# Relation layer of a four-layer graph network: waits between the indirect gathers of a half-turn

## The chip, the cores and the metric

The kernel runs on one NeuronCore of a Trainium2 chip as one program. The metric is the device time of an execution in microseconds; the median of three executions of the kernel before is 9646.02 us.

## The reference

Four graph layers follow one another on 6250 nodes of 64 features and 206250 edges that are sorted by destination. Each is added to its input. The change is in the last, the relation layer:

```python
    def _L3_gnn_ref(x, edge_index, edge_type, W_rel, W_self, b_self):
        ...
        out = x @ W_self.T + b_self
        src = x[edge_index[0]]
        msg = jnp.zeros((src.shape[0], W_rel.shape[1]), dtype=x.dtype)
        for r in range(W_rel.shape[0]):
            msg = msg + jnp.where((edge_type == r)[:, None], src @ W_rel[r].T, 0.0)
        out = out.at[edge_index[1]].add(msg)
        return jax.nn.relu(out)
    ...
    h = jnp.maximum(_layernorm(x, axis=-1), 0.0)
    x = x + _L3_gnn_ref(h, edge_index, edge_type_3, L3_gnn_W_rel, L3_gnn_W_self, L3_gnn_b_self)
```

## The kernel before

An earlier stage has written `relation_table` to HBM: for each node and each of three relations one row of 64 floats, the node's features times that relation's matrix. The relation layer then needs, for each edge, one row of that table, and running sums of those rows along the edges of each partition, so that a node's sum can be read at its last edge.

The 206250 edges lie as 128 partitions by T columns. A **half-turn** handles HALF = 26 columns, in one of two buffers (h = 0 or 1); a loop turn has two half-turns, and LP = 31 turns make 62 half-turns. Five engines run side by side in one block, each with a loop of its own, joined by semaphores alone:

- **POOL** (GpSimd) waits until ACT has staged the indices of the half-turn (`s_idx`), then issues NGA = 21 indirect gathers, one per column, each of 128 rows of 256 bytes, into `rows_l3_h` (line 3027). All 21 count on one semaphore, `s_rows[h]`, and are issued without a wait between them.
- The other ND = 5 columns are not gathered. **PE** makes them by dense one-hot products: five tiles of 21 matmuls each (line 3232), with small transposes and products by the relations' weights between them (lines 3242 and 3252), that **DVE** masks and sums (lines 3144 to 3172).
- **ACT** builds the one-hots (lines 2980 and 2983). In `body` it waits for the 21 gathers and for the dense rows, turns the 26 columns by feature into PSUM (lines 2993 to 2995), and only then stages the indices of the half-turn two on (line 2967). So the gathers of half-turn n + 2 start when half-turn n has been turned, and half-turn n + 1's gathers lie a whole period ahead of their use.
- **DVE** scans the turned columns (line 3179); ACT copies the result back (line 3003); **SP** stores it to `running_sums`, 832 KB per half-turn (line 3048), and loads the rows of codes for coming one-hots (line 3043).

Two other places gather in the same way. The mean layer (second of the four; line 1295) gathers from `h_table` in half-turns of 12 columns, GP = 12, and it already waits, ahead of each gather, for the landing of the gather two back:

```python
                        for u in range(GP):
                            if u > 1:
                                e.wait_ge(s_grow[s][u % 2], i * 8 * GP + 16 * (u // 2))
                                e.sem_inc(s_gpace, 1)
                            e.indirect_dma_start(grow[s][:, u, :], None, h1_d,
```

The attention layer (third; line 1600) gathers without such waits.

`retire(sems)` clears and frees semaphores behind a barrier of all engines. The first layer's semaphores (`l0_...`) are never freed in the kernel before.

Of the kernel before, what the change touches and what calls it, by code (L numbers as in the profile page):

```python
# [23 lines left out]
NACC = 4  # L24
# [122 lines left out]
def build(nc, x, src, dst, edge_attr, edge_type, w0a, b0a, w0b, b0b, w1, b1, watt, att_s, att_d, batt, wf1, bf1, wf2,  # L147
# [57 lines left out]
    with top:  # L205
# [3 lines left out]
        def sem(name, into=None):  # L209
            if into is None:  # L210
                return top.enter_context(nc.semaphore(name))
            into.append(nc.alloc_semaphore(name))
            return into[-1]

        def retire(sems):
            nc.clear_and_free_semaphores(sems)
            nc.all_engine_barrier()
# [384 lines left out]
        with ExitStack() as ctx:  # L602
# [22 lines left out]
            def borrow(k, n, dt=f32):  # L625
# [15 lines left out]
            s_attr = [sem(f"l0_attr{h}") for h in range(2)]  # L641
            s_stage, s_psrc, s_eq, s_sum, s_val, s_hot, s_hist, s_dup, s_tgt, s_vfree, s_acc = (
                sem(f"l0_{n}") for n in ("staged", "src_rows", "equal", "summed", "values", "onehots", "hist",
                                         "dup", "targets", "val_free", "pace"))
            s_high, s_left, s_spread, s_z, s_dig, s_digits = (
                sem(f"l0_{n}") for n in ("high_parts", "rests", "spread", "z_added", "digits_staged", "digits"))
            s_add = [sem(f"l0_acc{k}") for k in range(NACC)]
            s_init, s_tail, s_pack = sem("l0_init"), sem("l0_tail"), sem("l0_packed")
            s_away, s_gap = sem("l0_digits_negated"), sem("l0_digit_distances")
            s_srow = [sem(f"l0_src_rows_loaded{h}") for h in range(2)]  # L650
            s_turn, s_turnc, s_turnst = (sem(f"l0_{n}") for n in ("src_turned", "src_turned_copied", "src_turned_stored"))
# [335 lines left out]
        with ExitStack() as ctx:  # L987
# [205 lines left out]
            retire(retired0)  # L1193
# [1692 lines left out]
        with ExitStack() as ctx:  # L2886
# [39 lines left out]
            s_rows = [sem(f"l3_rows{h}", l3_sems) for h in range(2)]  # L2926
# [36 lines left out]
            with nc.Block() as block:  # L2963
                @block.scalar
                def _(e):
# [20 lines left out]
                    def body(i, h, more):  # L2986
# [3 lines left out]
                        e.wait_ge(s_rows[h], i * 16 * NGA + 16 * NGA)  # L2990
# [27 lines left out]
                @block.gpsimd  # L3018
                def _(e):
                    with e.Fori(0, LP) as i:  # L3020
                        for h in range(2):
                            hh = i * 2 + h

                            e.wait_ge(s_idx, hh + 1)
                            e.sem_inc(s_pace, 1)
                            for r in range(NGA):
                                e.indirect_dma_start(g[h][:, r, :], None, y3_d,  # L3027
                                                     bass.IndirectOffsetOnAxis(ap=idx[h][:, r:r + 1], axis=0))\
                                 .then_inc(s_rows[h], 16)
# [335 lines left out]
```

## Time and profile before

| | us |
|---|---|
| median of three executions | 9646.02 (9627.27 to 9649.23) |
| span of the profiled execution | 9754.5 |
| relation layer: first to last gather start of line 3027 | 7024.7 to 9642.7 |
| POOL busy, whole span | 5337.6 |
| PE matmul busy, whole span | 6607.5 |

The profiled execution has no time beside its span; its span is 108.5 us, 1.1%, over the median of the unprofiled executions. POOL's busy time counts an indirect gather for some 0.94 us, the time in which its descriptors are made; the transfer goes on after it.

### The profile page before, as it was taken

Reading aid. Unit: us, or ns where it says so; the run is one execution under the profiler, and the core shown is the slowest. Engines: PE = TensorE matmul, PEld = TensorE weight load, DVE = VectorE, ACT = ScalarE, POOL = GpSimd, SP = SyncE. Lnnn points to the kernel's source line nnn. Section 1 sums busy time; section 2 is a strip of 40 time slices with the busy share of each in tenths; the row PEclk is TensorE's granted clock in tenths of the full one; section 3 lists DMA queues with packets and bytes.
Section 4 is the critical chain, followed back from the end, with each engine's and each line's share of the span. In section 5 each row is a group of like instructions: output and inputs, shape, how many; then the busy total and the mean of one; then the engine's idle time right before and its main releaser. Section 6 shows DMA issues by size and latency. Waiting matters only on the chain. (4 is left out here: it accounts for less than half of the span.)

```text
span 9754.5 us, 145261 instructions
## 1 busy us (share of the span) xinstructions
PE 6607.5 (68%) x38830; PEld 4546.4 (47%) x38831; DVE 6236.8 (64%) x16834; ACT 4860.4 (50%) x11241; POOL 5337.6 (55%) x4893
## 2 busy tenths in 40 slices
PE   6988888875888852555555555557767666666665
PEld 3545545544777741445454444557533333333332
DVE  7999999986888832666676666668633333333333
ACT  5877777754777721333333333333334444444442
POOL 5888888873555545455555545551344444444444
PEclk9999999987888955555655555555577788888777
DMA  5444444441111112222222222222111111111111
GB/s 120 73 75 70 72 75 70 72 76 41 21 20 21 21 41 38 44 43 45 45 46 44 45 43 45 44 45 75 51 38 43 45 46 46 46 46 43 41 41 46
DMA packets 626461, 487.11 MB, mean 50 GB/s; under 512 B 513289, under 2 KB 530030, under 8 KB 616344
## 3 DMA queue, kind: packets, MB, share of 16 engines
q0 software_dynamic: 281600, 185.95, 15.9%
q1 hardware_dynamic: 342455, 293.43, 10.2%
q10 hardware_dynamic: 2304, 6.55, 0.3%
q8 instruction: 41, 0.67, 0.0%
q14 instruction: 61, 0.50, 0.0%
HBM read 303.43 MB, written 182.13 MB: 50 GB/s over the span
## 5 line engine op out<-in xcount | busy, mean ns | idle before, releaser
L1600 POOL DMA_INDIRECT tile_rows<-att_row_table,src_by_tile x1620 | 1528.4, 943 | 1413.6 <-PE banks L2269 763.7
L3027 POOL DMA_INDIRECT rows_l<-relation_table,idx x1302 | 1246.4, 957 | 1390.5 <-ACT idx L2967 1012.3
L976 POOL DMA_INDIRECT acc<-val,idx x1116 | 1722.6, 1544 | 378.9 <-issue 319.9
L3232 PE MATMUL banks<-h_parts,dense_onehot 128*128 128x448 bf16 x6510 | 1511.3, 383 | 553.0 <-issue 518.2
L2269 PE MATMUL banks<-tile_rows,prob 128*128 x4032 | 910.4, 402 | 1386.3 <-ACT prob L2210 595.5
L747 PE MATMUL banks<-part 128*128 128x490 bf16 (+1 forms) x7440 | 1569.6, 366 | 217.9 <-DVE part L830 209.8
L2269 PEld LDWEIGHTS banks<-tile_rows,prob 128*128 128x128 f32 x4032 | 831.8, 307 | 1480.6 <-issue 1480.3
L3232 PEld LDWEIGHTS banks<-h_parts,dense_onehot 128*128 128x128 bf16 x6510 | 643.0, 103 | 1334.6 <-issue 854.1
L747 PEld LDWEIGHTS banks<-part 128*128 128x128 bf16 x7440 | 694.3, 97 | 996.0 <-DVE part L830 270.4
L3144 DVE TENSOR_TENSOR h_nodes<-banks,dense_mask_j 128x448 f32<-128x448 f32 x310 | 192.9, 622 | 1476.3 <-remote 910.1
L2210 ACT COPY prob<-banks 128x1024 f32<-128x1024 f32 x252 | 255.0, 1012 | 1307.8 <-DMA quad_sums<-run 1076.4
L2318 DVE TENSOR_TENSOR banks<-banks,piece_att_dst 128x1024 f32<-128x1024 f32 x252 | 310.2, 1231 | 895.9 <-remote 877.9
L1295 POOL DMA_INDIRECT gathered_rows<-h_table,gathered_index x600 | 575.8, 960 | 545.3 <-issue 295.7
L906 ACT ACTIVATE digit_distance<-iota_row,dst_digits_negated 128x128 bf16<-128x128 f32 (+1 forms) x3224 | 868.7, 357 | 2.2 <-ACT dst_digits_negated L895 0.2
L1350 DVE TENSOR_SCALAR hot_src_lo<-columns_bf,codes 128x128 bf16<-128x128 bf16 x2300 | 613.6, 269 | 134.0 <-ACT codes L1414 59.4
L1453 ACT CAST counts<-banks 128x784 bf16<-128x784 f32 x650 | 522.2, 815 | 301.2 <-PE banks L1502 188.2
L830 DVE SCALAR_TENSOR_TENSOR part<-banks,src_digits,part 128x490 bf16<-128x490 f32 x992 | 671.2, 718 | 0.0
L1351 DVE TENSOR_SCALAR hot_code<-columns_bf,codes 128x196 bf16<-128x196 bf16 x2300 | 647.6, 285 | 0.0
L3003 ACT COPY run<-sums_by_feature 128x1664 f32<-128x1664 f32 x62 | 213.4, 3441 | 866.5 <-DVE sums_by_feature L3179 562.7
L2367 DVE SCALAR_TENSOR_TENSOR kept_l<-kept_l,fade,banks 128x65 f32<-128x65 f32 x2016 | 565.7, 281 | 117.9 <-issue 58.2
L1527 PE MATMUL banks<-counts,h_parts 128*128 128x208 bf16 x4900 | 630.0, 275 | 4.4 <-issue 4.2
L2196 ACT ACTIVATE edge_logit<-banks 128x1024 f32<-128x1024 f32 x252 | 257.8, 1023 | 569.8 <-DVE banks L2318 383.3
(449 smaller groups left out, 12370.0 us busy)
## 6 DMA issues: line engine op xcount, KB each, us to landing
src_rows<-src_by_column SPq DMA_DIRECT2D x63, 1152.0 KB
piece_sums<-kept_l SPq DMA_DIRECT2D x252, 264.0 KB
running_sums<-run SPq DMA_DIRECT2D x62, 832.0 KB
attr<-in_edge_attr SPq DMA_DIRECT2D x61, 624.0 KB
tile_rows<-att_row_table,src_by_tile POOLq DMA_INDIRECT x1620
rows_l<-relation_table,idx POOLq DMA_INDIRECT x1302
dense_code_rows<-src_by_column SPq DMA_DIRECT2D x62, 320.0 KB
acc<-val,idx POOLq DMA_INDIRECT x1116
```

The source lines that it names most:

```text
L747: last = e.matmul(ps[a][:, 0:ZW[a]], place0[(h * NZ + m) % 2][:, a, :], spread0[(h * NZ + m) % 2][n].rearrange("p b f -> p (b f)")[:, 0:ZW ...
L830: last = e.scalar_tensor_tensor(spread0[b][n], bc(ps[7][:, 0:ZB].unsqueeze(2), [P, ZB, W0]), dig[h][:, m, ZA:ZA + 1], bc(t.unsqueeze(1), [ ...
L906: last = e.activation(gap[n][:, r - a, :], iota[:, 0:w], ACT.Square, bias=away[n][:, r:r + 1])
L976: e.indirect_dma_start(acc_d[k], bass.IndirectOffsetOnAxis(ap=idx[h][:, r:r + 1], axis=0), val[h][:, r, :], None, compute_op=ALU.add).then ...
L1295: e.indirect_dma_start(grow[s][:, u, :], None, h1_d, bass.IndirectOffsetOnAxis(ap=gidx[s][:, u:u + 1], axis=0))\
L1350: e.tensor_scalar(hlo[slot(q)][:, u, :], cols[:, 0:P], code[s][:, 0, n:n + 1], None, ALU.is_equal)
L1351: last = e.tensor_scalar(hcd[slot(q)][:, u, :], cols[:, :], code[s][:, 1, n:n + 1], None, ALU.is_equal)
L1527: last = e.matmul(ps[4 + 1 - s][:, 0:BN * HT], parts4[:, m // 2, m % 2 * 2 * D:(m % 2 + 1) * 2 * D], table[1 - s][:, :, m // 2 * BN:(m // ...
L1600: e.indirect_dma_start(to, None, hx_d, bass.IndirectOffsetOnAxis(ap=src_col[:, t:t + 1], axis=0))\
L2269: last = e.matmul(summed(r), prob[u % 2][:, r, :], flat[:, bass.ds(cols[r], W1)], start=True, stop=True)
L3027: e.indirect_dma_start(g[h][:, r, :], None, y3_d, bass.IndirectOffsetOnAxis(ap=idx[h][:, r:r + 1], axis=0))\
L3232: last = e.matmul(ps[4 + b][:, 0:WJ], hot[h][:, k, m * P:(m + 1) * P], parts3[:, n, k * WJ:(k + 1) * WJ], start=(k == 0 and n == 0), stop= ...
```

## The change

In the relation layer POOL waits, ahead of gathers 2 to 20 of a half-turn, until the gather two back has landed. For this the gathers of a half-turn count in turn on two semaphores, even ones on `s_rows[h][0]` (11 of the 21) and odd ones on `s_rows[h][1]` (10). ACT's wait for all 21 becomes two waits. To have semaphores enough, those of the first layer are now collected in a list and freed with others at the end of that layer's last block.

```diff
-            s_rows = [sem(f"l3_rows{h}", l3_sems) for h in range(2)]
+            s_rows = [[sem(f"l3_rows{h}_{n}", l3_sems) for n in range(2)] for h in range(2)]
+            LANDED = [-(-NGA // 2), NGA // 2]
...
-                        e.wait_ge(s_rows[h], i * 16 * NGA + 16 * NGA)
+                        for n in range(2):
+                            e.wait_ge(s_rows[h][n], i * 16 * LANDED[n] + 16 * LANDED[n])
...
                             for r in range(NGA):
+                                if r > 1:
+                                    e.wait_ge(s_rows[h][r % 2], i * 16 * LANDED[r % 2] + 16 * (r // 2))
+                                    e.sem_inc(s_pace, 1)
                                 e.indirect_dma_start(g[h][:, r, :], None, y3_d,
                                                      bass.IndirectOffsetOnAxis(ap=idx[h][:, r:r + 1], axis=0))\
-                                 .then_inc(s_rows[h], 16)
+                                 .then_inc(s_rows[h][r % 2], 16)
...
-            s_attr = [sem(f"l0_attr{h}") for h in range(2)]
+            l0_sems = []
+            s_attr = [sem(f"l0_attr{h}", l0_sems) for h in range(2)]
...
-            retire(retired0)
+            retire(l0_sems + retired0)
```

On POOL, the relation layer's loop turn reads before as follows (the destination, then the table and the indices; `x20` stands for twenty more of the same):

```order
L3020 ISA
L3027 DMA rows_l3_0<-relation_table,idx0 128x64 [waits l3_staged]
L3027 DMA rows_l3_0<-relation_table,idx0 128x64 x20
L3024 REGISTER_ALU
L3027 DMA rows_l3_1<-relation_table,idx1 128x64 [waits l3_staged]
L3027 DMA rows_l3_1<-relation_table,idx1 128x64 x20
L3020 REGISTER_ALU
L3020 COMPARE_AND_BRANCH
```

The start of the same loop turn on POOL now:

```order
L3023 ISA
L3033 DMA rows_l3_0<-relation_table,idx0 128x64 [waits l3_staged]
L3033 DMA rows_l3_0<-relation_table,idx0 128x64
L3031 ISA
L3033 DMA rows_l3_0<-relation_table,idx0 128x64 [waits l3_rows0_0]
L3031 ISA
L3033 DMA rows_l3_0<-relation_table,idx0 128x64 [waits l3_rows0_1]
L3031 REGISTER_ALU
L3033 DMA rows_l3_0<-relation_table,idx0 128x64 [waits l3_rows0_0]
```

The first two gathers of a half-turn follow each other as before; each later one waits for a landing, and in half-turns of buffer 0 a register instruction stands between them as well. The gathers of buffer 1 have the waits without the register instruction.

On ACT, at `body` of buffer 0, before:

```order
L2983 ACTIVATE dense_onehot0<-h_nodes,dense_one 128x1280 [waits l3_gaps]
L2990 ISA
L2991 ISA [waits l3_rows0]
L2992 REGISTER_ALU [waits l3_dense_rows]
L2993 COPY banks<-sums_by_feature 128x64 [waits l3_scanned]
```

and now:

```order
L2985 ACTIVATE dense_onehot0<-h_nodes,dense_one 128x1280 [waits l3_gaps]
L2993 ISA
L2993 ISA [waits l3_rows0_0]
L2994 ISA [waits l3_rows0_1]
L2995 REGISTER_ALU [waits l3_dense_rows]
L2996 COPY banks<-sums_by_feature 128x64 [waits l3_scanned]
```

One wait has become two, at the same place; what follows is as it was. PE, DVE and SP have the same instructions as before in this layer.

## Rows read from the trace of the kernel before

**Rows 1.** The page's span and its queues of instruction loads.
```profile
span 9754.5 us, 145261 instructions
...
q8 instruction: 41, 0.67, 0.0%
q14 instruction: 61, 0.50, 0.0%
```

**Rows 2.** The gathers by source line: count, min/median/max ns, first and last start.
```profile
L3027 POOL DMA_INDIRECT rows_l<-relation_table,idx x1302: 938/944/7818, 7024.7 to 9642.7; - x186
```

**Rows 3.** What PE waited for, 7105 to 9640 us: total, times, longest.
```profile
PE banks L3232 <- issue: 506.7, 323, 3.2
```

**Rows 4.** Timeline of PE in one half-turn: start, length, count, idle before.
```profile
7667.36 4.15 PE L3232 MATMUL banks<-h_parts,dense_onehot 128*128 128x448 bf16 x21
7671.43 0.65 PE L3242 MATMUL banks<-ident,h_nodes 128*64 128x128 f32 x4
...
7687.29 1.69 PE L3232 MATMUL banks<-h_parts,dense_onehot 128*128 128x448 bf16 x8
7690.24 0.35 PE L3232 MATMUL banks<-h_parts,dense_onehot 128*128 128x448 bf16 x1 [1.26 <-issue]
...
7704.98 2.34 PE L3232 MATMUL banks<-h_parts,dense_onehot 128*128 128x448 bf16 x6 [0.17 <-issue]
7708.19 0.59 PE L3252 MATMUL banks<-w_again,h_nodes 64*128 64x192 f32 x2 [0.87 <-DVE h_nodes L3156]
7708.71 4.14 PE L3232 MATMUL banks<-h_parts,dense_onehot 128*128 128x448 bf16 x21
```

**Rows 5.** Timeline of POOL, the same half-turn.
```profile
7675.23 0.94 POOL L3027 DMA_INDIRECT rows_l<-relation_table,idx  x1 [16.91 <-ACT idx L2967]
7676.48 0.94 POOL L3027 DMA_INDIRECT rows_l<-relation_table,idx  x1 [0.30 <-issue]
...
7700.18 0.94 POOL L3027 DMA_INDIRECT rows_l<-relation_table,idx  x1 [0.30 <-issue]
7716.26 0.94 POOL L3027 DMA_INDIRECT rows_l<-relation_table,idx  x1 [15.13 <-ACT idx L2967]
```

**Rows 6.** Windows: PE, PEld, DVE, ACT, POOL busy, clock, DMA share, GB/s.
```profile
7681.00:7689.00 8.00, 7.64 (x40) 3.89 (x39) 4.57 (x4) 0.00 (x0) 5.87 (x8) 1.00 0.14 25
7690.00:7696.00 6.00, 1.23 (x3) 0.20 (x2) 0.05 (x1) 5.88 (x4) 4.58 (x5) 0.79 0.38 125
```

**Rows 7.** Timeline of PE, then of POOL, in other half-turns.
```profile
8600.16 0.35 PE L3232 MATMUL banks<-h_parts,dense_onehot 128*128 128x448 bf16 x1 [0.38 <-issue]
...
8615.67 3.23 PE L3232 MATMUL banks<-h_parts,dense_onehot 128*128 128x448 bf16 x9 [0.87 <-issue]
...
9299.51 6.61 PE L3232 MATMUL banks<-h_parts,dense_onehot 128*128 128x448 bf16 x21
...
8585.89 0.94 POOL L3027 DMA_INDIRECT rows_l<-relation_table,idx  x1 [15.73 <-ACT idx L2967]
```

**Rows 8.** What PE waited for in the mean layer, 2326 to 3450 us.
```profile
PE banks L1502 <- issue: 23.8, 27, 3.0
PE banks L1527 <- issue: 4.2, 11, 0.9
```

**Rows 9.** Timeline of POOL in the mean layer.
```profile
2911.67 0.95 POOL L1295 DMA_INDIRECT gathered_rows<-h_table,gathered_index  x1 [8.77 <-ACT gathered_index L1410]
2912.92 0.94 POOL L1295 DMA_INDIRECT gathered_rows<-h_table,gathered_index  x1 [0.31 <-issue]
2914.86 0.94 POOL L1295 DMA_INDIRECT gathered_rows<-h_table,gathered_index  x1 [0.99 <-DMA gathered_rows<-h_table,gathered_index]
...
2930.45 0.94 POOL L1295 DMA_INDIRECT gathered_rows<-h_table,gathered_index  x1 [0.30 <-issue]
```

**Rows 10.** Windows in the mean layer, columns as in rows 6.
```profile
2380.00:2460.00 80.00, 70.33 (x673) 61.10 (x672) 70.30 (x386) 59.18 (x116) 45.59 (x48) 0.91 0.12 23
```

**Rows 11.** Window over 59 half-turns, columns as in rows 6.
```profile
7125.00:9617.00 2492.00, 1675.52 (x7423) 779.07 (x7422) 894.42 (x1188) 1098.30 (x948) 1174.01 (x1244) 0.80 0.17 44
```

**Rows 12.** The page's DMA issues: count and KB each.
```profile
running_sums<-run SPq DMA_DIRECT2D x62, 832.0 KB
```

More of the change, by code:

```diff
@@ L640, in build @@
             src_z = src0f[:, 0:T].rearrange("p (h r) -> p h r", r=HALF)[:, :, HS:HALF]
-            s_attr = [sem(f"l0_attr{h}") for h in range(2)]
+            l0_sems = []
+            s_attr = [sem(f"l0_attr{h}", l0_sems) for h in range(2)]
             s_stage, s_psrc, s_eq, s_sum, s_val, s_hot, s_hist, s_dup, s_tgt, s_vfree, s_acc = (
-                sem(f"l0_{n}") for n in ("staged", "src_rows", "equal", "summed", "values", "onehots", "hist",
+                sem(f"l0_{n}", l0_sems) for n in ("staged", "src_rows", "equal", "summed", "values", "onehots", "hist",
                                          "dup", "targets", "val_free", "pace"))
             s_high, s_left, s_spread, s_z, s_dig, s_digits = (
[L646 to L651, printed above, removed]
+                sem(f"l0_{n}", l0_sems) for n in ("high_parts", "rests", "spread", "z_added", "digits_staged", "digits"))
+            s_add = [sem(f"l0_acc{k}", l0_sems) for k in range(NACC)]
+            s_init, s_tail, s_pack = (sem(f"l0_{n}", l0_sems) for n in ("init", "tail", "packed"))
+            s_away, s_gap = (sem(f"l0_{n}", l0_sems) for n in ("digits_negated", "digit_distances"))
+            s_srow = [sem(f"l0_src_rows_loaded{h}", l0_sems) for h in range(2)]
+            s_turn, s_turnc, s_turnst = (sem(f"l0_{n}", l0_sems) for n in ("src_turned", "src_turned_copied", "src_turned_stored"))
             assert TT * P >= T + HALF > (TT - 1) * P and 12 < TT < 17 and TT * P <= HS * P
```

## The prediction
> **What bounds the kernel now.** I read first where the relation layer lies and how long a half-turn takes, then the timelines of PE and POOL over one half-turn, then the same two engines in the mean layer, which already has the waits that the change adds.
>
> The span of the profiled execution is 9754.5 us [rows 1]. The 1302 gathers of line 3027 are 62 half-turns of 21; first and last start are 7024.7 and 9642.7 us [rows 2]. The last half-turn's first gather lies 20 steps of 1.25 us (25 us) ahead of the last one, so 61 periods fill 2593 us: 42.5 us per half-turn. The one of the timeline is typical: its second tile starts at 7667.36 and the next half-turn's at 7708.71 [rows 4], 41.35 us.
>
> In that time PE is the engine that the others wait for, but it does not work all the time. From 7667.36 to 7687.29 four of its five tiles go by with what stands between them: 19.9 us, each tile some 4.07 us from its start to the next row's [rows 4]. The fifth starts at 7687.29 and is over only at 7708.19, 20.9 us where 4.1 would do. In it single matmuls stand 2 to 3 us apart, and the idle time ahead of them is put down to "issue": PE waited for nothing that the profile shows. Inside a tile the program has no wait at all. Over the layer that is 506.7 us of idle in 323 gaps, a little more than five a half-turn [rows 3], and more goes into the wide steps between them. Without the crawl PE's half-turn would be 41.35 - 20.9 + 4.1 = 24.6 us.
>
> What goes on beside the crawl: POOL starts its gathers at 7675.23, steps by 1.25 us, and starts the last at 7700.18 [rows 5]. The crawl begins 15 us after the first gather (7690.24) and ends 4.8 us after the start of the last (7704.98) [rows 4, 5]. Another half-turn, whose first gather starts at 8585.89, has its first gap ahead of 8600.16 and its last ahead of 8615.67 [rows 7]: 14.3 and 29.8 us after the first gather, where the one above has 15.0 and 29.75. The place in PE's program is not the same in the two (after the 8th matmul of the tile there, after the 5th here). So it goes by the gathers' time, not by PE's code. The DMA engines are not full at its onset: their share is 0.14 before, and 0.38 in the crawl because SP's store of 832 KB [rows 12] falls into it [rows 6]. The granted clock falls after PE has gone quiet (1.00, then 0.79, then 0.50), that is from 2.4 to 1.2 GHz, so the clock is a result and makes the recovery a little slower.
>
> **What the mean layer says.** There POOL already waits for the landing of the gather two back. In its whole loop the matmuls of line 1527 lost 4.2 us to "issue", those of line 1502 23.8 us [rows 8], though PE is fed as densely (673 matmuls in 80 us, busy 70.3, with 48 gathers beside them [rows 10], so 1.67 us per gather, kept up over the 80 us). There is no crawl. The gathers are of the same kind: 128 rows of 256 bytes and 0.94 us each.
>
> **The change part by part.** *The waits on POOL.* In the mean layer a gather whose landing is waited for starts 3.19 us after the one two back (2911.67 to 2914.86), and from the first gather of one half-turn to the first of the next are 18.78 us for 12 gathers [rows 9]: five pairs and two unpaced steps of 1.25 us, so a pair takes (18.78 - 2.5) / 5 = 3.26 us. With 21 gathers there are ten pairs and one step: 10 x 3.26 + 1.25 = 33.85 us for POOL per half-turn, where it was 26.2. The register instructions stand in the mean layer too and are in that pair. Queued behind the waits are only the other gathers.
>
> *What the store adds.* SP's store of 832 KB takes DMA time in the relation layer, and the mean layer has nothing of its size. The window with the store shows 125 GB/s over 6 us [rows 6]; a gather caught in it lands later, and then POOL waits longer. Bounds: nothing, if it only fills idle engines; or 5 us, if no gather lands during the store (832 KB at 125 GB/s is 6.7 us, less the 1.6 that a gather takes anyway). I take 2 us, since the share in that window is 0.38 and so mostly free. POOL then needs 35.85 us a half-turn.
>
> *Whether anybody waits for the later gathers.* The gathers of half-turn n + 2 start when n has been turned; POOL now idles 15 to 17 us ahead of each half-turn for ACT's indices [rows 5], so its own 7.6 to 9.6 us more are covered even at today's period, and the rows are needed a whole period after their start. If the period shrinks, that cover goes: POOL becomes the bound at 35.85 us, with its indices staged well ahead.
>
> *What is removed.* If the crawl goes, as in the mean layer, PE needs 24.6 us, ACT 1098 / 59 = 18.6 us and DVE 894 / 59 = 15.2 us of work per half-turn [rows 11], all below 35.85. PE would then idle some 10 us a half-turn, and the clock would fall there; a tile at the lower clock takes 6.61 us instead of 4.15 [rows 4, 7]; with three of five tiles slow PE is at 24.6 + 3 x 2.46 = 32 us, still below POOL. So the new period is POOL's, 35.85 us.
>
> *The semaphores of the first layer.* They are cleared with others behind a barrier that is there before: at most a microsecond. ACT's second wait passes with the first: nothing.
>
> **The sum.** The first two half-turns are bound by the layer's start and I leave them out; 59 periods go from 42.3 us (what is left of the 2593 us) to 35.85: 6.45 x 59 = 380 us less. The span would be 9754.5 - 380 = 9374 us. The profiled span stands 1.1% over the median, so off the median go 376 us: 9646 - 376 = 9270 us. That the unprofiled time is only 108 us shorter also says that the crawl (62 times some 16 us) is not made by profiling.
>
> **The rule that speaks against it.** By POOL's rows alone the gathers are hidden already, with 15 us to spare [rows 5], and a wait between them gains nothing. The Trainium skill, "DMA: Bandwidth & Descriptors", section on rules for kernel authors, says to issue a DMA early and wait on its semaphore late, so that its fixed cost overlaps; by it the change can only cost, and at best nothing. The mean layer's rows decide it for me the other way.
>
> **Rivals.**
> 1. *The crawl goes by the gathers' rate, and is only shortened.* At 1.25 us a step it starts after 11 or 12 gathers; if it builds up whenever gathers come faster than about 1.7 us apart, the paced stream of 1.71 us (35.85 / 21) is near that edge, and a short crawl or slower gathers put the half-turn at 37.5 to 41 us. For it: the onset needs a backlog. Against: 1.67 us per gather over 80 us in the mean layer [rows 10]. Saving 1.3 to 4.8 us x 59: 9363 to 9570 us, say 9450. Chance 0.13.
> 2. *The crawl is PE's own code loading and has nothing to do with the gathers.* A loop turn of PE is taken back at a branch, and the code behind it would have to come again. Then the half-turn stays at 42 us and the waits hide in POOL's idle time: 9646 us. Against: the crawl's place follows the gathers, and the queues of instruction loads hold 41 and 61 packets in the whole span [rows 1], not some for each of 62 half-turns. The skill's page "Runtime: NRT & Kernel Launch", section on instruction fetch, says that a taken branch to code outside the window forces such a load; no row here shows one in this loop. Chance 0.05.
> 3. *Slower: the crawl lasts as long as gathers are in flight, from some 14 us after the first.* Then POOL's longer burst makes it longer: 33.85 - 26.2 = 7.6 us more crawl, of which PE gets a little done: a half-turn of some 48.5 us, 6.2 x 59 = 366 us more: 10010 us. It decides from a half-turn of 42.3 us on, that is when 17.7 us of crawl are left over PE's 24.6. Against: the mean layer has gathers in flight nearly all the time. Chance 0.10.
> 4. *The store delays no gather*: POOL at its floor of 33.85 us, 8.45 x 59 = 499 us less: 9152 us. This belongs to my forecast's range.
>
> **How the numbers follow.** My forecast (crawl gone, POOL the bound) has a chance of 0.72; its own range is 9130 to 9350 us (a little below the floor of rival 4, and a store that costs 3.4 us). With rivals 1, 2 and 3 at 0.13, 0.05 and 0.10, the range that leaves out no more than 2 in 10 goes from 9110 to 9560 us: it takes in rival 1 nearly whole and leaves out rivals 2 and 3. Faster by over 0.3% (about what a measurement of this kernel tells from no change): 0.84; within: 0.06; slower: 0.10.
>
> **What the new profile would show.** Right: the gathers of the relation layer start in pairs some 3.2 to 3.5 us apart, with a landing as what ended POOL's idle time; POOL no longer waits for ACT's indices by 15 us; PE's idle ahead of line 3232 put down to "issue" falls from 507 us to a few tens; 35 to 36.5 us from half-turn to half-turn; ACT waits for the gathers' landing instead of the dense rows. Wrong: gaps of 2 us inside a tile that remain (rivals 1 to 3), or a stream of gathers slower than 1.8 us each, or a period set by PE at the lower clock.

## The result, and the profile after

The changed kernel takes 9264.18 us (median of 4 executions, 9257.33 to 9268.39); the kernel before, timed beside it on the same chip, 9640.17 us (4 executions, 9627.27 to 9649.23). The ratio is 0.9607, with a 95% interval of 0.9594 to 0.9621: 376 us faster. The forecast was 9270 us.

The profiled execution of the changed kernel has a span of 9262.3 us. The gathers by source line, with what POOL waited for ahead of them and who waited for them, answer to [rows 2]:

```profile
L3033 POOL DMA_INDIRECT rows_l<-relation_table,idx x1302: 942/946/4982, 6931.8 to 9169.2; - x186
its engine sat idle before it (us, times) until:
  DMA rows_l<-relation_table,idx: 528.1, 433
  issue: 461.9, 868
  ACT idx L2969: 17.9, 1
```

From the first to the last gather the layer took 2618.0 us before [rows 2]; it takes 2237.4 us now, 380.6 us less. POOL has stopped waiting for ACT's indices: once in the whole layer, where 15 to 17 us of each half-turn went there [rows 5]. It waits for landings instead.

What PE waited for from 7105 to 9200 us (engine, what it was to write and its line, then what ended the wait: total us, times, longest) answers to [rows 3]:

```profile
PE banks L3238 <- ACT dense_onehot L2985: 523.6, 55, 12.6
...
PE banks L3238 <- issue: 12.1, 1, 12.1
```

The 323 gaps put down to "issue" are gone; the one that is left stands ahead of the first matmul of a tile, not inside one. In their place stands one wait of some 9.5 us a half-turn, for the one-hots that ACT builds. ACT is late with them because it waits itself. What ACT and POOL waited for, from 7105 to 9130 us:

```profile
ACT banks L2996 <- DMA rows_l<-relation_table,idx: 956.7, 56, 20.0
...
POOL rows_l L3033 <- DMA rows_l<-relation_table,idx: 468.5, 386, 3.5
```

ACT stands 17 us of each half-turn waiting for gathered rows, and the next one-hots lie behind that wait in its program. POOL's stream of gathers sets the period, and PE idles at the end of that chain. PE's timeline over one half-turn answers to [rows 4]:

```profile
7605.80 0.43 PE L3248 MATMUL banks<-ident,h_nodes 128*64 128x128 f32 x2
...
7607.00 4.14 PE L3238 MATMUL banks<-h_parts,dense_onehot 128*128 128x448 bf16 x21
...
7621.19 4.15 PE L3238 MATMUL banks<-h_parts,dense_onehot 128*128 128x448 bf16 x21
7625.26 0.65 PE L3248 MATMUL banks<-ident,h_nodes 128*64 128x128 f32 x4
7634.97 5.63 PE L3238 MATMUL banks<-h_parts,dense_onehot 128*128 128x448 bf16 x21 [9.05 <-ACT dense_onehot L2985]
7640.52 0.43 PE L3248 MATMUL banks<-ident,h_nodes 128*64 128x128 f32 x2
```

Every tile goes by unbroken, in 4.15 us, or mostly 5.5 to 6.9 us for the one behind the idle time, where the clock has fallen (the granted clock is 0.70 from 7635 to 7640 us, and 1.00 from 7607 to 7625). The pattern repeats after 34.7 us (7605.80 to 7640.52); over the layer, from the third half-turn on, the mean period is 36.0 us (before: 42.1). The whole stretch answers to [rows 11]:

```profile
7125.00:9200.00 2075.00, 1485.39 (x7064) 741.27 (x7064) 862.77 (x1133) 1040.96 (x897) 1145.03 (x1204) 0.85 0.21 51
```

The mean granted clock is 0.85 where it was 0.80, although PE idles.

POOL's timeline in the same half-turn answers to [rows 5]:

```profile
7601.48 0.96 POOL L3033 DMA_INDIRECT rows_l<-relation_table,idx  x1 [1.02 <-DMA rows_l<-relation_table,idx]
7602.77 0.95 POOL L3033 DMA_INDIRECT rows_l<-relation_table,idx  x1 [0.33 <-issue]
7604.74 0.95 POOL L3033 DMA_INDIRECT rows_l<-relation_table,idx  x1 [1.03 <-DMA rows_l<-relation_table,idx]
7607.85 0.95 POOL L3033 DMA_INDIRECT rows_l<-relation_table,idx  x1 [2.17 <-DMA rows_l<-relation_table,idx]
...
7643.36 0.95 POOL L3033 DMA_INDIRECT rows_l<-relation_table,idx  x1 [2.58 <-DMA rows_l<-relation_table,idx]
```

The gathers go in pairs: 3.26 us from 7601.48 to 7604.74, as in the mean layer [rows 9]. About once a half-turn one wait is longer, mostly 2.1 to 3.6 us instead of 1.0, some 5 us after SP has issued its store of `running_sums` (7603.03 and 7638.34, the long waits ahead of 7607.85 and 7643.36).

### The profile page after: what moved, and what is told of

It reads as the page before. It is cut to its first block and busy times, and to the rows that moved or that the text cites. A ratio compares the mean times of both kernels' runs of the same rounds, so it can differ in the third digit from the quotient of the medians.

```text
span 9262.3 us, 147096 instructions
## 1 busy us (share of the span) xinstructions
PE 6435.8 (69%) x38830; PEld 4515.4 (49%) x38831; DVE 6237.3 (67%) x16834; ACT 4851.9 (52%) x11241; POOL 5349.5 (58%) x4893
## 5 line engine op out<-in xcount | busy, mean ns | idle before, releaser
L3238 PE MATMUL banks<-h_parts,dense_onehot 128*128 128x448 bf16 x6510 | 1406.6, 376 | 574.2 <-ACT dense_onehot L2985 562.1
L2197 ACT ACTIVATE edge_logit<-banks 128x1024 f32<-128x1024 f32 x252 | 258.1, 1024 | 675.0 <-DVE banks L2319 521.5
```

Source lines behind the costliest of these rows:

```text
L3238: last = e.matmul(ps[4 + b][:, 0:WJ], hot[h][:, k, m * P:(m + 1) * P], parts3[:, n, k * WJ:(k + 1) * WJ], start=(k == 0 and n == 0), stop= ...
```

## The experiments

Twelve kernels ran, in four groups, each group on one chip beside the kernel before (9643.49 us in the first group, free_only to slow_step and late_waits; 9640.34 us in the second, half_partitions, every_third, every_fourth and group_waits_attention; the others are told with their groups). Ratios are to the kernel before of the same group, with a 95% interval. "Period" is the mean time from half-turn to half-turn, from the third on, of the profiled execution. The crawl is told in two ways, both in one stretch (7105 to 8970 us, 43 to 57 half-turns) of all profiles. "Gaps" are PE's idle times ahead of the matmuls of the tiles, put down to "issue". "Lost" is all idle time of PE in the layer's products that ends by "issue" or by DVE, and so leaves out the wait for ACT's one-hots alone; it is given for one half-turn:

| kernel | gathers start every | gaps, total us | lost, us | period us | ratio |
|---|---|---|---|---|---|
| before | 1.25 us | 281, 442.4 | 13.1 | 42.1 | 1 |
| free_only | 1.25 us | 161, 238.7 | 13.3 | 41.7 | 1.0005 |
| half_partitions | 1.21 us | 230, 340.0 | 14.7 | 43.2 | 1.0092 |
| three_back | 1.25 us | 158, 204.2 | 12.7 | 40.9 | 0.9917 |
| slow_step | 1.27 us | 158, 138.1 | 10.4 | 38.0 | 0.976 |
| late_waits | 11 at 1.25, then pairs | 104, 58.0 | 8.1 | 36.3 | 0.963 |
| every_fourth | 4 at 1.25, then a landing | 67, 29.6 | 6.3 | 33.3 | 0.943 |
| every_third | 3 at 1.25, then a landing | 8, 44.4 | 1.2 | 32.9 | 0.9413 |
| the change | pairs | 1, 12.1 | 0.2 | 36.0 | 0.9607 |

The number of gaps alone misleads: before and free_only have the same program in this layer, 281 gaps and 161, but lose the same, since the crawl often falls between tiles, where the wait is put down to "issue" ahead of the small products or to DVE. In every_fourth the longest such row is

```profile
PE banks L3258 <- DVE h_nodes L3162: 148.8, 37, 7.2
```

The 8 gaps of every_third and the one of the change all stand ahead of the first matmul of a tile; inside the tiles these two have none. That the waits for DVE belong to the crawl shows in fills_only, below: in a group of runs without it, this measure finds less than 1 us in the whole layer.

### Which part of the change does it: the freed semaphores or the waits

**free_only** is the kernel before with the first layer's semaphores freed, and no waits:

```diff
-            s_attr = [sem(f"l0_attr{h}") for h in range(2)]
+            l0_sems = []
+            s_attr = [sem(f"l0_attr{h}", l0_sems) for h in range(2)]
...
-            retire(retired0)
+            retire(l0_sems + retired0)
```

> The kernel before with one part of the change alone: the first layer's semaphores are freed early; the gathers have one semaphore per buffer and no waits between them. Theory (the gain is from the waits between the gathers): no change, ratio 0.998 to 1.002, half-turns of the relation layer at 41 to 42.5 us, and matmuls 2 to 3 us apart inside tiles, from some 14 us after the first gather to 4.5 us after the start of the last. Rival (freeing or renumbering semaphores matters): the time moves part of the way to 9264 us.

9652.53 us, ratio 1.0005 [0.9995, 1.0014]. The freeing costs and brings nothing; all of the gain is the waits'.

### Waits as such, or the rate that they leave

Theory A is that the crawl comes from an unbroken stream of gathers at 1.25 us, so that waits help only as far as they slow or break it. Theory B is that any waits for landings do, because they bound how many gathers are in flight.

**three_back** waits for the gather three back, by three semaphores instead of two:

```diff
-                                if r > 1:
-                                    e.wait_ge(s_rows[h][r % 2], i * 16 * LANDED[r % 2] + 16 * (r // 2))
+                                if r >= 3:
+                                    e.wait_ge(s_rows[h][r % 3], i * 16 * LANDED[r % 3] + 16 * (r // 3))
```

> The changed kernel with waits for the gather three back, counted by three semaphores, so up to three in flight. A gather's landing frees its waiter 3.2 us after its start, and three steps of 1.25 us are 3.75 us, so the waits pass at once except beside SP's store, and the gathers step by 1.25 us as before the change. Theory A (PE's crawl goes by the rate of the gathers, a backlog that builds at one gather per 1.25 us): the crawl is back, half-turns of 40 to 42 us, ratio to the kernel before 0.99 to 1.00. Theory B (the crawl comes from POOL running on without waits, or from more than some two in flight at the store): the crawl is gone, POOL needs 26 to 28 us per half-turn and PE about 25 to 28, so half-turns of 27 to 30 us, ratio 0.91 to 0.93 (some 8800 to 8950 us).

9576.65 us, 0.9917 [0.9893, 0.9941]. POOL's timeline in one half-turn, and PE's:

```profile
7390.53 0.94 POOL L3033 DMA_INDIRECT rows_l<-relation_table,idx  x1 [5.71 <-ACT idx L2969]
7391.77 0.94 POOL L3033 DMA_INDIRECT rows_l<-relation_table,idx  x1 [0.30 <-issue]
7393.02 0.95 POOL L3033 DMA_INDIRECT rows_l<-relation_table,idx  x1 [0.30 <-DMA rows_l<-relation_table,idx]
7394.27 0.94 POOL L3033 DMA_INDIRECT rows_l<-relation_table,idx  x1 [0.30 <-DMA rows_l<-relation_table,idx]
```

```profile
7402.48 1.69 PE L3238 MATMUL banks<-h_parts,dense_onehot 128*128 128x448 bf16 x8
7405.31 0.35 PE L3238 MATMUL banks<-h_parts,dense_onehot 128*128 128x448 bf16 x1 [1.14 <-issue]
...
7410.21 0.53 PE L3238 MATMUL banks<-h_parts,dense_onehot 128*128 128x448 bf16 x1 [3.15 <-issue]
7413.01 0.53 PE L3238 MATMUL banks<-h_parts,dense_onehot 128*128 128x448 bf16 x1 [2.27 <-issue]
...
7420.01 2.02 PE L3238 MATMUL banks<-h_parts,dense_onehot 128*128 128x448 bf16 x5 [0.17 <-issue]
```

The waits pass at once: the landing of the gather three back is there when POOL comes to ask, the pause is 0.30 us as without a wait, and the step stays 1.25 us. The crawl comes as before, its first gap 14.8 us after the first gather (7390.53 to 7405.31). In a half-turn of this kernel no more than three gathers can be in flight, and PE crawls all the same (12.7 us lost in a half-turn, 13.1 before): B falls. every_third, below, lets three be in flight too, and is nearly free of the crawl.

**late_waits** keeps the change's waits only for gathers 11 to 20:

```diff
-                                if r > 1:
+                                if r > 10:
```

> The changed kernel with the waits for the gather two back only from gather 11 on; gathers 0 to 10 step by 1.25 us. POOL needs 11 x 1.25 + 5 x 3.25 = 30 us per half-turn plus some 1.5 us beside the store. Theory A (a backlog that builds at 1.25 us a step and overflows after 11 or 12 gathers): at gather 11 it is just short of overflow and the paced rest lets it drain or keeps it there, so there is no crawl or a short one, half-turns of 31 to 34 us, ratio 0.92 to 0.955 to the kernel before. Theory B (waits anywhere are enough): no crawl either, 31 to 32 us. If PE crawls for 10 us or more, half-turns of 36 us or more, both need another form: then what matters is how long gathers go on without a pause.

9292.29 us, 0.963 [0.9614, 0.9647]. This lies outside what either theory expected (31 to 34 us, 0.92 to 0.955). Eleven gathers in a row start something of a crawl (104 gaps of 0.56 us on the mean, where they were of 1.6 us before; 8.1 us lost in a half-turn), and with the pairs behind them it is milder. From first to last gather POOL needs 30.4 us here and the period is 36.3, so POOL is no longer the bound: what it saves on the first eleven is lost to the crawl again.

**slow_step** has no waits for landings, but three one-column fills on POOL between gathers:

```diff
                             for r in range(NGA):
+                                for n in range(3 if r else 0):
+                                    last = e.memset(idle[:, (h * HALF + r) * 3 + n:(h * HALF + r) * 3 + n + 1], 0.0)
                                 e.indirect_dma_start(g[h][:, r, :], None, y3_d,
```

> The kernel before (no wait for a landing) with three one-column fills on POOL between the gathers, into a tile that nothing reads; at about 0.12 us each with their dispatch they should bring the step from 1.25 to 1.5 to 1.8 us. Theory A (rate): with the step near 1.6 us the crawl is gone or short, half-turns of 33 to 37 us, ratio 0.95 to 0.97, like the change itself. Theory B (it takes the waits for landings): the crawl stays, from some 14 us after the first gather, and the half-turn is 42 us or more, ratio 1.00 to 1.04.

9419.22 us, 0.976 [0.9744, 0.9776]. It was meant to slow the stream and did not: the fills fit into the 0.30 us that POOL stands between two gathers, and the step is 1.27 us. Still the crawl costs less (10.4 us lost in a half-turn). POOL's timeline at its onset suggests why:

```profile
7732.02 0.18 POOL L3032 MEMSET idle_row<- 128x1 f32 x3
7732.35 0.94 POOL L3035 DMA_INDIRECT rows_l<-relation_table,idx  x1 [0.15 <-issue]
7733.30 0.11 POOL L3032 MEMSET idle_row<- 128x1 f32 x1
7734.17 0.10 POOL L3032 MEMSET idle_row<- 128x1 f32 x1 [0.76 <-issue]
7735.57 0.10 POOL L3032 MEMSET idle_row<- 128x1 f32 x1 [1.30 <-issue]
7735.82 0.94 POOL L3035 DMA_INDIRECT rows_l<-relation_table,idx  x1
```

POOL's own small instructions are held up as PE's are (0.76 and 1.30 us between fills that stand 0.1 us apart otherwise). By that POOL's stream slows itself when the crawl begins (its steps are 1.40 us on the mean, where the median is 1.27), which may be what shortens the crawl; no run tests that. The crawl is so not a matter of PE alone; it also says nothing for or against a slower stream, since the stream was not slower.

### Rows and bytes, or instructions

**half_partitions** gathers 64 rows instead of 128 with each instruction:

```diff
-                                e.indirect_dma_start(g[h][:, r, :], None, y3_d,
-                                                     bass.IndirectOffsetOnAxis(ap=idx[h][:, r:r + 1], axis=0))\
+                                e.indirect_dma_start(g[h][0:P // 2, r, :], None, y3_d,
+                                                     bass.IndirectOffsetOnAxis(ap=idx[h][0:P // 2, r:r + 1], axis=0))\
```

> The kernel before (no waits between the gathers), in which each gather of the relation layer moves 64 rows instead of 128; the rows of partitions 64 to 127 are not gathered and stay zero, so half of the gathered edges are left out of the relation layer. The count of instructions on POOL is the same. If POOL's time for a gather stays near 0.94 us, the step stays at 1.25 us with half of the descriptors and bytes: theory D (the crawl goes by descriptors or bytes) expects no crawl, PE the bound, half-turns of 25 to 29 us and a time of 8750 to 8950 us; theory P (it goes by POOL's instructions, whatever they move) expects the crawl as before, 41 to 42 us and 9640 us. If the gather takes half as long on POOL, the step is some 0.8 us: D expects the crawl's onset at gather 18 or so, P at gather 11.

9728.01 us, 1.0092 [1.0062, 1.0122]. Half the rows and half the bytes: a gather takes 0.90 us instead of 0.94, the step is 1.21 us, the crawl begins after some 12 gathers (its first gap is 14.8 us after the first gather in the middle half-turn, 15.0 before) and is no weaker (14.7 us lost in a half-turn). So it does not go by rows or bytes. The DMA packets were not halved: the trace has 32 for each gather in both kernels, 16 of 2048 bytes (1024 here) and 16 of 4 bytes. So it goes by how close gather instructions follow each other, or by something that each does however many rows it has, its 32 packets among them.

### The best spacing

The change holds POOL at pairs, 33.9 us a half-turn at best, and POOL is now the bound. If only unbroken bursts matter, fewer waits are better.

```diff
-                                if r > 1:
+                                if r and r % 3 == 0:
```

is **every_third**; **every_fourth** has `r % 4`.

> The changed kernel, with POOL waiting for the gather two back only ahead of every third gather (3, 6, ... 18): per three gathers 1.25 + 3.2 = 4.45 us, 1.48 us per gather, POOL 31.2 us per half-turn plus about 1.5 us beside the store; not more than three gathers in a row without a wait. Theory A (the crawl goes by a rate that can be kept up, somewhere between one gather in 1.25 and one in 1.67 us): if 1.48 us is slow enough there is no crawl and the half-turn is 32.7 us, 3.3 x 60 = 200 us under the changed kernel, ratio to the kernel before 0.94. If it is too fast, gaps inside tiles come back and the half-turn is 35 us or more, ratio 0.96 or over. Theory B (any wait two back, often enough, stops it): 32.7 us.

> As every_third, with a wait ahead of every fourth gather: 2.5 + 3.2 = 5.7 us per four, 1.43 us per gather, POOL 30.2 us plus 1.5. Theory A: nearer to the edge; if the crawl goes by the mean rate, more of it than in every_third, and a half-turn no shorter. If the edge is under 1.43 us the half-turn is 31.7 us, ratio 0.935.

9075.94 us, 0.9413 [0.9394, 0.9431], and 9102.14 us, 0.943 [0.9407, 0.9454]. A wait ahead of every third gather gives two steps of 1.25 us and one of some 1.9 (1.47 us on the mean, the store apart), no crawl to speak of (no gap inside a tile, 1.2 us lost in a half-turn) and a period of 32.9 us. With every fourth it is three of 1.25 and one of 1.95 (1.43 us on the mean), and part of the crawl comes back: 6.3 us lost in a half-turn, and POOL, which is done sooner, waits for ACT's indices again (164.3 us in all, 17.9 in every_third). The intervals overlap, so the two are not told apart in time; more gathers between waits bring nothing more. Both beat the change by some 2%.

### The other unpaced layer

The attention layer gathers in groups of 8 and waits only for the group four back. **group_waits_attention** is the change and, there, a wait for the group just before:

```diff
-                        if g >= TSEMS:
-                            e.wait_ge(s_tile[g % TSEMS], 16 * QUAD * (g // TSEMS) + 16)
-                            e.sem_inc(s_pace, 1)
+                        e.wait_ge(s_tile[(g - 1) % TSEMS], 16 * QUAD * ((g - 1) // TSEMS + 1) + 16)
+                        e.sem_inc(s_pace, 1)
```

> The changed kernel, and in the attention layer POOL waits, ahead of each group of 8 gathers, until the group before has landed (before: four groups back): 7 x 1.25 + 3.2 = 11.95 us per 8, 1.49 us per gather, 1620 gathers in 2420 us at least, in a stage of 2940 us. Theory A (bursts at 1.25 us make the other engines crawl there too, as the gap of 14.3 us on PE beside 16 gathers in a row says): the stage becomes shorter, 50 to 400 us, total 8850 to 9210 us. Rival (the attention layer is bound by its own chain through PE, ACT and DVE, and the bursts only use slack): 9264 us within 0.3%, or a few tens of us more.

9021.83 us, 0.9359 [0.9343, 0.9374]. The attention layer's gathers take 2658 us from first to last where they took 2902 with the change alone. What PE waited for there, 3600 to 6250 us, with the change alone:

```profile
PE banks L2270 <- issue: 319.5, 105, 12.2
```

and with the group waits:

```profile
PE banks L2269 <- issue: 70.5, 53, 4.4
```

The gaps put down to "issue" fall by 249 us, and the stage by 244 us. What DVE waited for there for no cause that the profile names ("remote") falls too, but most of it stays. First with the change alone, then with the group waits:

```profile
DVE banks L2319 <- remote: 785.5, 122, 48.3
DVE banks L2318 <- remote: 628.3, 190, 5.0
```

This is the fastest kernel measured beside a kernel before of 9640 us.

### A group of runs without a crawl

The third group was meant to put the good parts together. **thirds_and_groups** is every_third with the attention layer's group waits; **mean_thirds_too** has in addition a wait ahead of every third gather in the mean layer, instead of each:

```diff
-                            if u > 1:
+                            if u and u % 3 == 0:
```

**fills_only** is the kernel before with eight one-column fills between gathers, to slow the stream to 1.4 us with no landing waited for:

```diff
+                                for n in range(8 * r, 8 * r + 8 if r else 0):
+                                    last = e.memset(idle[:, n:n + 1], 0.0)
```

> The two paced forms together: the relation layer waits ahead of every third gather (9076 us alone), the attention layer waits group by group (9022 us on top of the change, so 242 us of its own). If the two gains lie in separate layers and add: 9264 - 188 - 242 = 8834 us, ratio to the kernel before 0.916. Rival: one gives back part of the other: over 8870 us.

> As thirds_and_groups, and the mean layer too waits ahead of every third gather instead of every one from the third on. POOL's 12 gathers then take 3 x 4.45 + 2 x 1.25 + 1.25 = 17.1 us instead of 18.8 there; where POOL is the bound of that layer (about half of its 50 half-turns, by its periods of 18.7 us) up to 1.7 us each are gained, 20 to 50 us in all. Rival: the layer's PE and DVE, which issue small instructions closely, meet the crawl at 1.48 us per gather and the time gets worse by some tens of us.

> The kernel before with eight one-column fills between the gathers and no wait for a landing; three took the step from 1.25 only to 1.27 us, since each costs 0.06 us and 0.15 us of the pause between gathers was free. Eight should give 0.94 + 0.15 + 0.46 = 1.55 us, 32 us of POOL per half-turn. Theory A (rate of the gathers alone): no crawl, or hardly any, half-turns of 32.5 to 35 us, ratio 0.94 to 0.96. Theory B (what helps is that POOL really waits for landings): the crawl comes after 11 gathers as before, and POOL's own fills are caught in it, half-turns of 38 us or more, ratio 0.975 or over.

The three expectations were worked out for a kernel before of 9640 us, but in this group it took 7557.93 us (7 executions, 7554.87 to 7558.82), over a fifth less than in the two groups ahead. Beside it thirds_and_groups took 8339.97 us, 1.1037 [1.1018, 1.1055]; mean_thirds_too 8323.03 us, 1.1013 [1.0995, 1.1032]; fills_only 7771.38 us, 1.0284 [1.0266, 1.0301]. Only one comparison inside the group can still be made: waits ahead of every third gather in the mean layer took 17 us off, just short of the 20 to 50 us expected (943.9 us from first to last gather of that layer instead of 959.1). The eight fills brought the step to 1.41 us, not to 1.55. What PE waited for in the relation layer of fills_only, 6000 to 7600 us:

```profile
PE banks L3240 <- ACT dense_onehot L2985: 207.5, 54, 7.0
```

It is the only row: no gap is put down to "issue". PE's timeline shows whole tiles beside gathers that go on at 1.41 us without a break:

```profile
6800.13 4.15 PE L3240 MATMUL banks<-h_parts,dense_onehot 128*128 128x448 bf16 x21
...
6822.81 6.86 PE L3240 MATMUL banks<-h_parts,dense_onehot 128*128 128x448 bf16 x21 [3.77 <-ACT dense_onehot L2985]
```

Its attention layer, which is as in the kernel before, takes 2034 us from first to last gather; the changed kernel's, the same program there, takes 2902 us. So in this group unpaced gathers did not disturb the other engines.

More than the unpaced gathers is different, though. The stages by first to last gather, in us, each row one program:

| stage | groups with a kernel before of 9640 us | third group | fourth group (below) |
|---|---|---|---|
| first layer | 2066.7 (before) | 2068.1 (fills_only) | 2067.6 |
| mean layer, waits two back | 1114.0 (before), 1059.8 (the change) | 959.0 (fills_only), 959.1 (thirds_and_groups) | 1175.0 |
| attention layer as before | 2940.8 (before), 2902.5 (the change) | 2034.2 (fills_only) | 2950.1 |
| attention layer, group waits | 2658.1 (group_waits_attention) | 2453.9 (thirds_and_groups) | |
| relation layer, the change | 2237.4 (the change) | | 2208.4 |
| relation layer, every third | 2042.4 (every_third) | 2067.1 (thirds_and_groups) | |

The first layer and the paced relation layer take nearly the same in every group. The mean layer does not, though it has the waits two back in all of these kernels: from the first gather of a half-turn to the first of the next it takes 18.7 and some 25.5 us in turn in the kernel before, and mostly 18.5 us each time in fills_only. In the kernel before, ACT and DVE stood there (2326 to 3440 us) for no cause that the profile names:

```profile
ACT counts L1453 <- remote: 96.9, 37, 4.8
DVE hot_src_lo L1350 <- remote: 48.3, 24, 5.0
DVE quad_running L1361 <- remote: 43.1, 19, 3.7
```

fills_only has no such row, and thirds_and_groups has none for DVE in the attention layer either, where group_waits_attention has 628 us. So waits two back did not keep the mean layer free of disturbance, and the group waits left the attention layer 204 us longer than it takes here. Whether it is the same crawl is not shown: no run takes the mean layer's waits away.

In the relation layer of this group the period is POOL's own: fills_only has 29.9 us (21 steps of 1.41 are 29.6), and the kernel before, which is 213 us faster, comes to 29.9 - 213 / 59 = 26.3 us, 21 steps of 1.25. The kernel before itself has no profile in this group, so that is worked out, not read. Here every wait costs: every_third's form has 33.3 us a half-turn. Because there is no crawl to remove, fills_only does not say whether a stream of 1.41 us without landing waits would be free of it elsewhere.

**change_again** is the change itself once more (only a comment differs), to have it timed in that condition:

> The changed kernel itself, unaltered, timed once more against the kernel before on one chip. The last three runs shared a chip on which the kernel before takes 7558 us where the chips of the earlier runs gave 9640 to 9643 us. Theory C (the crawl does not occur on that chip, and POOL's gathers are the bound of the relation layer there): the fills took half-turns of 29.9 us and 213 us over the kernel before, so 3.6 us each, which puts the half-turn of the kernel before at 26.3 us, the 21 steps of 1.25 us; the waits of the change make it some 35.9 us, so (35.9 - 26.3) x 60 = 576 us more: 8130 us, ratio 1.075, if this run meets such a chip. If it meets a chip on which the kernel before takes 9640 us, the change is at 9264 us again, ratio 0.961. Rival: the chip with 7558 us differs in something else, and there the change is within 1% of the kernel before, or faster.

The condition was not met again. The kernel before took 9842.34 us (11 executions, 9806.11 to 9906.14) and the change 9387.48 us (9380.76 to 9404.32), 0.9529 [0.9499, 0.9558]. It repeats the gain, a little larger, and its relation layer has no gap at all inside the tiles (period 35.6 us). Its profiled execution is 140 us longer than the first one of the change (9402.6 against 9262.3), and 115 of them lie in the mean layer (table above). The chip has the same number as that of the third group; whether it is the same piece is not known. The change alone was never timed where the crawl is absent; by its 36.0 us a half-turn against 26.3, 59 x 9.7 = 572 us more, it would be at some 8130 us there, 7 to 8% slower than before (an estimate).

## Why the prediction was right, point by point

**The crawl is the gathers' doing and goes when they are paced.** Right, with main forecast and measurement 6 us apart. The gaps fell from 323 to one, and PE's lost time from 13.1 to 0.2 us a half-turn. free_only shows that the waits alone did it.

**The mean layer has no crawl.** This premise was read too well. The rows of PE [rows 8] are small, but those of ACT and DVE above show 188 us of waits without a named cause, and every second half-turn there is some 7 us longer than where the crawl is absent. The 80 us of [rows 10] lie in a good stretch: 1.67 us per gather there, 1.86 over the layer (1114.0 us for 600 gathers). The waits did clear the relation layer, so the conclusion held, but this evidence for it was weaker than it looked; to that extent it was luck.

**POOL becomes the bound, 33.85 us a half-turn.** Right. The pair is 3.26 us, as in the mean layer, and POOL waits for indices once in the layer.

**The store adds 2 us.** This was a choice between 0 and 5. Measured: the mean period is 36.0 us, so what the store and all other small delays add is 36.0 - 33.85 = 2.2 us.

**59 periods save 6.45 us each, 380 us.** From first to last gather 380.6 us are gone. That the two agree so closely is luck in part. The period before was 42.1 us, not 42.3 (the last half-turn's gathers took 31.8 us instead of the 25 assumed), and the new one is 36.0, so the 59 periods save 6.12 x 59 = 361 us. The first two half-turns, which the sum left out, save 21 us (100.3 to 79.1). And the profiled execution of the kernel before was long here too. Against free_only, whose layer takes 2591.7 us and whose program is that of before in it, the gathers' stretch is 354 us shorter, and another 27 us lie behind the last gather's start (9538.5 to the end at 9659.0, 120.5 us, against 93.1 now), where a crawl ended in one and not in the other: 381 us again, but in two pieces, of which the sum named one.

**The profiled span stands 1.1% over the median, so the saving is scaled by it.** This step had no ground. The changed kernel's profiled span (9262.3) is that of its timed executions. The 9754.5 us of before were one long execution, with 93 us of the difference ahead of the relation layer (7024.7 against 6931.8; free_only starts the layer at 6946.8), 54 of them in the mean layer. The step moved the saving from 380 to 376 us, so nothing came of it.

**PE at 24.6 to 32 us stays below POOL.** Right: one tile of five runs slow, not three, and the clock is higher on the whole.

**Rival 1, that the crawl goes by the rate and would only be shortened.** Half right, and worth more than 0.13 as a mechanism: the crawl does need a stream dense enough. But in the relation layer the edge lies at a faster stream than the change's, not at it: pairs (1.63 us on the mean, the store apart) and threes (1.47) lose 0.2 and 1.2 us a half-turn, fours (1.43) 6.3, eleven in a row 8.1. Whether it is the mean rate or the number without a break that counts, these runs do not tell apart. Its time, 9363 us or more, did not come.

**Rival 2, PE's own code loading.** Falls: with PE's program the same the gaps go from 281 to one by POOL's waits, and in slow_step POOL itself is caught. The Trainium skill, "Runtime: NRT & Kernel Launch", on instruction fetch, says that a taken branch forces a load where its target lies outside the window of code that the engine holds. Whether PE's does in this loop no run shows; the whole tiles of the profile after show no cost of one.

**Rival 3, that the crawl lasts as long as gathers are in flight.** Falls: gathers are in flight nearly all the time now, and there is none.

**The rule that spoke against the change.** Where the kernel before takes 9640 us, it loses: waiting early gained 4%, and 6% with waits ahead of every third gather. Where it takes 7558 us the two kernels paced in both layers are 10% slower, the way that rule points. The Trainium skill, "DMA: Bandwidth & Descriptors", rules for kernel authors (issue early, wait late) knows only the second case.

**What stays open.** Which resource PE's and POOL's instructions wait for in the crawl; why it needs some 12 gathers to begin, whatever their size; whether slowness alone would do without landings waited for; what holds ACT and DVE up in the mean layer in spite of its waits; and above all what made all of this absent in one group of runs. The prediction could not have told this last from its trace: in the profile of the kernel before the crawl goes through the whole layer, some five gaps a half-turn [rows 3].

## What to carry to other kernels

When an engine falls apart inside a stretch in which its program has no wait, with gaps put down to "issue", look at what POOL does at that time before looking at the engine: if indirect gathers run there without a break, wait for a landing ahead of every third one, and price it by POOL's own floor (21 gathers at 1.25 us are 26 us, with such waits some 31, and with SP's store 33), since POOL may become the bound. Count all the time that the engine loses, not only the gaps of one row, since the same crawl can fall between the tiles. Compare with the kernel before on the same chip and at the same time, in more than one place: the same edit was worth 4 to 5% here, and its stronger forms cost 10% where the crawl did not occur.

## What was not expected of the hardware

- In the crawl the distances between the starts of PE's instructions are close to multiples of 0.70 us: 7410.21, 7413.01, 7414.41, 7416.51, 7417.92, 7419.31 in three_back are 2.80, 1.40, 2.10, 1.41 and 1.39 us apart, 4, 2, 3, 2 and 2 times 0.70. Over the kernel before, 264 of the 355 distances of 1.2 to 4.5 us between tile matmuls lie within a tenth of a step of such a multiple. POOL's two held fills in slow_step are 1.40 us apart (7734.17 to 7735.57).
- A gather of 64 rows costs POOL 0.90 us, one of 128 rows 0.94 us: nearly all of it is per instruction.
- Between two gathers POOL stands 0.30 us for no wait that shows, and three one-column fills fit in for 0.02 us.
- The same mean layer, with its waits two back, took 959 us in one group of runs and 1059 to 1175 us in the others; the first layer took 2066 to 2070 us in all of them.
- One program took 7558, 9640 and 9842 us in different groups of runs, each time within about 1% in its group. Nothing in these runs tells ahead which it will be.
